# Joined value products, and products for the maxima behind the scores: an attention and expert kernel on one core

## The reference

```python
xn = layernorm(x)
# attention, 16 heads of 8 numbers
scores = Q @ K.T / sqrt(8) + 0.1 * influence     # influence = (xn We.T)(xn We.T).T, the same for all heads
attn   = softmax(scores)
att    = (attn @ V) @ Wo.T
# experts: the best 2 of 8 for every row
y      = w2[e] @ gelu(w1[e] @ xn + b1[e]) + b2[e]
out    = x + att + sum over the two experts of probability * y
```

## Time and profile before

| | before |
|---|---|
| median of 3 runs | 711.17 us |
| profiled execution | 710.7 us |
| its span, first to last instruction | 708.9 us |
| TensorE busy | 645.0 us, 91% |
| VectorE busy | 613.8 us, 87% |
| ScalarE busy | 540.8 us, 76% |
| GpSimd busy | 469.0 us, 66% |
| mean granted TensorE clock | 0.98 of 2.4 GHz |

### The profile page before, as it was taken

One profiled execution on the slowest core, in us unless ns is written; L12 is line 12 of the kernel. 1 busy time (PEld: TensorE's weight loads), 2 busy tenths in 40 slices (PEclk: granted clock), 3 DMA queues, 4 the chain that ended last, 5 costly groups with the idle time before them and its releaser, 6 DMA issues.

```text
span 708.9 us, 22900 instructions
## 1 busy us (share of the span) xinstructions
PE 645.0 (91%) x7800; PEld 431.6 (61%) x7800; DVE 613.8 (87%) x1106; ACT 540.8 (76%) x1123; POOL 469.0 (66%) x542
## 2 busy tenths in 40 slices
PE   0367899999999999879999999999999999999996
PEld 0254445555555555569999999999455555555553
DVE  8979899999899899758888888887999999999991
ACT  2583478888888888758888888888787887778785
POOL 8680478687677657125566566566688888878883
PEclk9996799999999999999999999999999999999999
DMA  9859566676686776564444454543576877788742
GB/s 249 305 161 338 150 160 180 179 204 167 178 199 178 184 183 172 148 109 100 101 106 102 101 96 110 103 99 79 142 169 174 191 186 187 175 189 195 179 112 76
DMA packets 162975, 113.71 MB, mean 160 GB/s; under 512 B 72624, under 2 KB 150448, under 8 KB 162864
## 3 DMA queue, kind: packets, MB, share of 16 engines
q1 hardware_dynamic: 153632, 90.63, 51.5%
q0 software_dynamic: 8192, 16.86, 9.8%
q10 hardware_dynamic: 1040, 4.76, 1.8%
HBM read 55.42 MB, written 47.19 MB: 145 GB/s over the span
## 4 chain that ended last, share of the span: by engine, by line
PE 62%; DVE 16%; SPq 9%; DMA 7%; issue 4%; ACT 1%; DVEq 0%; ACTq 0%
PE bank L1243 14%; PE mx L1232 13%; PE bank L1125 12%; PE bank L1103 10%; DVE mx L948 8%; PE mx L1137 6%; DMA stack<-qk_dram 4%; PE bank L1023 2%; PE bank L1185 2%; DVE A L783 2%; SPq L322 2%; DVE lo_qk L966 2%; DMA stack<-mT 2%; SPq L326 1%; PE bank L1154 1%
## 5 line engine op out<-in xcount | busy, mean ns | idle before, releaser
L700 ACT ACTIVATE A<-bank 128x512 f32<-128x512 f32 x502 | 278.0, 597 | 57.6 <-PE bank L1125 48.7
L948 DVE TENSOR_REDUCE mx<-mx 128x4 f16<-128x1024 f32 x256 | 302.5, 1205 | 18.4 <-PE mx L1137 15.9
L571 POOL TENSOR_SCALAR rows<-rows,slot_p 128x128 f32<-128x128 f32 x142 | 112.2, 800 | 99.0 <-DVE rows L999 99.0
L1125 PE MATMUL bank<-stack 113*128 113x256 f16 x1004 | 170.1, 276 | 1.8 <-ACT A L700 0.8
L557 POOL DMA_INDIRECT slots_x<-rows,pos x128 | 124.0, 969 | 50.9 <-PE bank L1125 30.0
L601 POOL DMA_INDIRECT rows<-slots_y,pos x128 | 122.0, 953 | 37.1 <-issue 18.2
L1103 PE MATMUL bank<-A,V 128*32 128x256 f32 x2048 | 137.1, 385 | 1.8 <-ACT A L700 1.7
L744 ACT ACTIVATE rows<-mx,b 128x256 f32<-128x256 f32 x284 | 111.5, 475 | 30.2 <-PE mx L1232 29.9
L1125 PEld LDWEIGHTS bank<-stack 113*128 113x128 f16 x1004 | 73.2, 97 | 89.6 <-ACT A L700 48.7
L993 DVE TENSOR_TENSOR rows<-rows 128x512 f16<-128x512 f32 x142 | 101.2, 714 | 24.5 <-ACT rows L748 22.1
L1243 PE MATMUL bank<-w,rows 128*128 x1704 | 108.4, 220 | 4.4 <-DVE rows L993 4.4
(11 more groups left out here) (142 smaller groups left out, 591.4 us busy)
## 6 DMA issues: line engine op xcount, KB each, us to landing
stack<-ctx_rest SPq DMA_DIRECT2D x64, 256.0 KB
stack<-qk_dram SPq DMA_DIRECT2D x128, 96.0 KB
slots_y<-rows SPq DMA_DIRECT2D x71, 128.0 KB, 2.1
qk_dram<-hi_qk SPq DMA_DIRECT2D x64, 128.0 KB
stack<-ctx_high SPq DMA_DIRECT2D x128, 64.0 KB
slots_x<-A ACTq DMA_DIRECT2D x1, 4644.0 KB, 19.8
w_stage<-in_w SPq DMA_DIRECT2D x8, 512.0 KB
qk_dram<-lo_qk SPq DMA_DIRECT2D x64, 64.0 KB
```

What stands on the lines that cost most here:

```text
L571: ins = pool.tensor_scalar(ye[n % 4][:, h, :], ye[n % 4][:, h, :], slot_p[:, n // 4 % 3, n % 4, h:h + 1], None, ALU.mult)
L700: act.activation(A[:, n % NA, :, :].rearrange("p h s -> p (h s)"), scores(k, n)[:, :], ACT.Exp, scale=SCALE).then_inc(s_xp, 1)
L948: dve.tensor_reduce(mx[:, a, 8 * qt:8 * qt + 8].rearrange("q (i e w) -> q i e w", i=2, e=2)[:, :, g % 2], MX[u % 2][:, :].rearrange("q (i ...
L1125: mm = pe.matmul(scores(k, n)[:, i * S:(i + 1) * S], stack[0:SHIFT + 1, par, h, 1, c * P:(c + 1) * P], stack[0:SHIFT + 1, par, h, 0, :], s ...
```

## The change

- The four groups of value products of a batch are issued in two joined pairs: groups 0 and 1 in unit 4 behind the scores, groups 2 and 3 in unit 0 of the next step, behind the scores and the output projection. (In the last step, k = 31, groups 0 to 2 stay in units 3, 5 and 7.)
- As exponentials live longer, the ring A has ten buffers in place of eight, and an exponential waits for the group that last read its buffer.
- On even units in which scores are computed, the two `plain` numbers come behind the scores and the values, not ahead of them.
- V has another layout: 48 columns for each of 16 pairs of heads, which two windows of 32 columns share, 768 columns in place of 1088. The weights of V are reordered on the host, and ScalarE's copy of V comes after the exponentials of unit 4, not of unit 3.

```diff
-NA = 8
-VB = 272
+NA = 10
+VP = 3 * 2 * DE // 2
...
-        V = sb("V", [P, 2, 4 * VB], F32)
+        V = sb("V", [P, 2, H * VP], F32)
...
-            at_ = VB * (2 * c + g % 2) - 16 * (g % 2) + 32 * (4 * (g // 2) + i)
+            at_ = VP * (8 * c + 4 * (g // 2) + i) + 16 * (g % 2)
             return V[:, par, at_:at_ + 32]
...
-                            if k != 0 or g >= 2:
-                                act.wait_ge(s_pv, 4 * b + g - 1)
+                            if 16 * b + n >= NA:
+                                act.wait_ge(s_pv, (16 * b + n - NA) // 4 + 1)
...
-                    if u == 3 and f["m"]:
+                    if u == 4 and f["m"]:
                         act.wait_ge(s_v, b1_ + 1)
...
-                    if f["m"] and u % 2 == 0:
+                    if f["m"] and u % 2 == 0 and not f["x"]:
                         for v in (u, u + 1):
                             plain(v)
                     for p in range(2):
...
                     if u == 0 and f["o"] and not closing:
-                        values(bo, paro, 3)
+                        for n in (2, 3):
+                            values(bo, paro, n)
...
-                    if u in ((3, 5, 7) if k == B - 1 else (2, 4, 6)) and f["x"]:
+                    if f["x"] and k == B - 1 and u in (3, 5, 7):
                         values(b, par, g - 1)
+                    if f["x"] and k != B - 1 and u == 4:
+                        for n in range(2):
+                            values(b, par, n)
+                    if f["m"] and u % 2 == 0 and f["x"]:
+                        for v in (u, u + 1):
+                            plain(v)
```

More of the change, by code:

```diff
@@ L184, in build @@
         stats = A[:, 0, :, :].rearrange("p h s -> p (h s)")[:, 0:NT * 6].rearrange("p (t s) -> p t s", s=6)
-        zeros = A[:, 1:NA // 2, :, :].rearrange("p n h s -> p (n h s)")[:, 0:ZROWS * RW // 2]
-        part_c = [A[:, NA // 2 + r, :, :].rearrange("p h s -> p (h s)").bitcast(F16).rearrange("p (a t) -> p a t", a=2) for r in range(4)]
+        zeros = A[:, 1:4, :, :].rearrange("p n h s -> p (n h s)")[:, 0:ZROWS * RW // 2]
+        part_c = [A[:, 4 + r, :, :].rearrange("p h s -> p (h s)").bitcast(F16).rearrange("p (a t) -> p a t", a=2) for r in range(4)]
         early = w12[:, :, :].rearrange("p a n -> p (a n)")
@@ L235, in head_values, with head_columns @@
         def head_values(par, c, g, i):
-            at_ = VB * (2 * c + g % 2) - 16 * (g % 2) + 32 * (4 * (g // 2) + i)
+            at_ = VP * (8 * c + 4 * (g // 2) + i) + 16 * (g % 2)
             return V[:, par, at_:at_ + 32]
+        def head_columns(par):
+            v = V[:, par, 0:DK]
+            return bass.AP(v.tensor, v.offset, [list(v.ap[0]), [VP, H], [32, 2], [1, DK]])
         s_x = [sem(f"s_x{q}") for q in range(4)]
@@ L485, in _ @@
             for par in range(2):
-                ins = pool.memset(V[:, par, :].rearrange("p (n j) -> p n j", n=4)[:, :, 0:256].rearrange("p n (j d) -> p n j d", d=32)[:, :, :, DK:DK + 1], 1.0)
+                ins = pool.memset(V[:, par, :].rearrange("p (n j) -> p n j", j=VP)[:, :, DK:VP:32], 1.0)
             ins.then_inc(s_post, 1)
@@ L694, in attend @@
                                 act.wait_ge(s_zero, 64)
-                            if k != 0 or g >= 2:
-                                act.wait_ge(s_pv, 4 * b + g - 1)
-                            if k == 0 and n == NA // 2:
+                            if 16 * b + n >= NA:
+                                act.wait_ge(s_pv, (16 * b + n - NA) // 4 + 1)
+                            if k == 0 and n == 4:
                                 for sm in s_cw:
                                     act.wait_ge(sm, 96)
-                            act.activation(A[:, n % NA, :, :].rearrange("p h s -> p (h s)"), scores(k, n)[:, :], ACT.Exp, scale=SCALE).then_inc(s_xp, 1)
+                            act.activation(A[:, (16 * b + n) % NA, :, :].rearrange("p h s -> p (h s)"), scores(k, n)[:, :], ACT.Exp, scale=SCALE).then_inc(s_xp, 1)
                     if u == 1 and f["p"]:
@@ L715, in attend @@
                             act.wait_ge(s_pv, 4 * b1_ - 4)
-                        act.activation(V[:, par1, :].rearrange("p (n j) -> p n j", n=4)[:, :, 0:256].rearrange("p n (j d) -> p n j d", d=32)[:, :, :, 0:DK],
-                                       MISC[:, 0:S].rearrange("p (n j d) -> p n j d", n=4, d=DK), ACT.Copy, scale=1 / WS).then_inc(s_vc, 1)
+                        act.activation(head_columns(par1), MISC[:, 0:S].rearrange("p (n e d) -> p n e d", e=2, d=DK), ACT.Copy, scale=1 / WS).then_inc(s_vc, 1)
                     if u == 2 and c_lo is not None:
@@ L1102, in values @@
                         for i in range(4):
-                            mm = pe.matmul(PV[32 * i:32 * i + 32, 0:S], head_values(pp, c, g, i), A[:, (4 * g + 2 * c + i // 2) % NA, i % 2, :],
+                            mm = pe.matmul(PV[32 * i:32 * i + 32, 0:S], head_values(pp, c, g, i), A[:, (16 * bb + 4 * g + 2 * c + i // 2) % NA, i % 2, :],
                                            start=(e == 0 and c == 0), stop=(e == 1 and c == 1))
@@ L1180, in attend @@
                     if u == 0 and f["o"] and closing:
-                        values(bo, paro, 3)
+                        for n in ((3,) if bo == B - 1 else (2, 3)):
+                            values(bo, paro, n)
                     if u == 0 and f["c"]:
@@ L1260 @@
     from concourse.bass_utils import run_bass_kernel_spmd
-    wv = np.asarray(L0_attn_Wv).reshape(2, 2, 4, DK, D).transpose(1, 0, 2, 3, 4).reshape(D, D)
+    wv = np.asarray(L0_attn_Wv).reshape(2, 2, 4, DK, D).transpose(0, 2, 1, 3, 4).reshape(D, D)
     wq, wk = (np.asarray(w).reshape(2, 2, 2, 2, DK, D).transpose(4, 0, 2, 1, 3, 5).reshape(D, D) for w in (L0_attn_Wq, L0_attn_Wk))
```

## The result

The changed kernel takes 825.97 us, the median of four runs (825.12 to 827.61); the kernel before, run beside it, 711.61. The ratio is 1.160, with a 95% interval of 1.156 to 1.165: slower by 114 us. The forecast was 811, range 775 to 860.

What follows compares the result with a forecast made beforehand. A loop through TensorE and VectorE was taken to bound the kernel, set by when each `plain` comes. Full steps add 87 us, partial ones 13, together 100 on 710.7: 811 us, range 775 to 860.

Steps and rivals of the forecast that it cites:

- the walk: One changed step timed product by product from plain 0: period 16.74 us, not 13.16 or 13.33; 811 us, chance 0.72.
- the two waits of the scratch bank: TensorE's projection waits for VectorE's addition into x (until 2.08), V's products for `lo_qk` (until 5.56), sharing one scratch bank.
- three of the ring: TensorE's second scores of units 4, 6 and 0 wait for exponentials; a bank's next score pair follows after 1.06 us.
- the loop: TensorE and VectorE waiting by turns close the period; before, via plain 1, plain 2 and maxima 2 to 7: 13.1 us.
- The links through the two tiles of maxima: `MX` has two tiles, so a `plain` waits for an earlier maximum: plain 1 for the maximum of plain 7.
- its signs: V copies 16 to 17 us apart; VectorE idle ahead of maxima 0 and 4, 1.5 to 2 us each; TensorE waits.
- The sum: Added time over all steps: 87 us in 25 full steps and 13 in six partial ones, together 100 us.
- The partial steps: Six steps at the stages' ends that lack some work, given 2.2 us each: 13 us.
- The scratch bank as a rival: Waits for the addition and `lo_qk` covered, only score ring and `MX` tiles hold TensorE: period 14.9, 760 us; chance 0.09.
- The clock as a rival: TensorE's clock falls each step at the joined values, doubling 1.7 us of work: 49 us more, 860 us; chance 0.12.
- The faster rival: TensorE's saved changes set the time: period falls to VectorE's 12.6 us, 696 us; chance 0.05.
- The edits at no cost: Ten buffers, V's new layout and its later copy, with loads and gathers, add no time; uncovered, the copy would cost 12 us.

Runs made afterwards that it cites:

- the order alone: Kernel before with one edit: on even units the products for the maxima come behind scores and values; groups, buffers, layout as before. 822.38 us, ratio 1.153.

## Why the prediction was right

**The order as the cause.** Shown: the order alone gives 109 us, the period answers as the walk has it to changes made at its links (the two waits of the scratch bank, and three of the ring, those three changed together), and the same work off the loop costs nothing. The links through the two tiles of maxima were read from the trace; no run changed them by themselves.

**The walk, link by link.** Counted from plain 0 at 641.28, the projection came at 2.17 (forecast 2.08), V's products at 5.69 (5.56), values at 7.43 (7.27), plain 4 at 9.29 (9.17), the output projection at 14.48 (14.25), the next plain 0 at 16.99 (16.74). No link failed: the walk was 0.09 us behind at the projection and 0.25 at the end of the step. The joined pair took 1.86 us (648.71 to 650.57), where 1.9 was taken. VectorE's gap of 0.56 us ahead of maximum 2 is in the walk too (3.19 to 3.71), though not among its signs.

**The sum.** 100 us forecast; the span grew by 117. Of the 17 us between them the lag of 0.25 us in 24 steps is 6. Every second step of the first stage took some 17.36 us, not 16.99: ScalarE's copies of the expert weights, which the walk left out, put off an exponential there, 0.37 us in six of the 13 steps, 2 us. One such copy, and the scores that wait behind it for 0.66 us:

```profile
146.13 1.05 ACT L730 ACTIVATE w<-w_stage 128x1024 f16<-128x1024 f32 x1
```

```profile
147.81 0.79 PE L1129 MATMUL bank<-stack 113*128 113x256 f16 x4 [0.66 <-ACT A L705]
```

Two of the 24 steps took 18.63 us by a fall of the clock, 3.3 us. The partial steps were put too low, 21 us (which takes in one full step) against 16; four more joined pairs stand there at the half clock (3.40, 3.33, 3.58 and 3.16 us where 1.93 is usual, 5.7 us together), so most of this is likely the clock too.

**The scratch bank as a rival.** Its price was right, 760 forecast and 763 measured once the two waits were taken away, and partly by luck: it took 14.9 us for every step, where the second stage had 14.75 and the first 14.68 and 15.82 by turns. The kernel as changed does wait at them.

**The clock as a rival.** It was given 0.12 and 49 us, a fall in each step. In the changed kernel it happened at six joined pairs of unit 4 (at 88.12, 105.31, 261.45, 562.05, 579.11 and 767.84 us), 9 us at most by the sum above, each at about the price forecast: a joined pair of 3.58 us where it is 1.93 otherwise, in a step of 18.63 us. TensorE at that place, and the granted clock ahead of it and in it:

```profile
579.11 3.58 PE L1107 MATMUL bank<-A,V 128*32 128x256 f32 x32
```

```profile
575.40:578.80 3.40, 1.61 (x17) 0.82 (x17) 3.32 (x5) 1.88 (x5) 2.93 (x3) 1.00 0.17 41
579.00:582.30 3.30, 3.30 (x34) 1.46 (x32) 0.31 (x2) 1.09 (x3) 2.84 (x3) 0.54 0.85 213
```

So both cases were partly true at once, and the forecast treated them as apart. The wait for the low half ahead of the fall at 579.11 was 1.31 us, longer than the usual 1.11, but ahead of the one at 261.45 it was 1.12; why some steps fall and others don't, no run here shows. Nor is the fall in the earlier trace rows the only one of the kernel before: its trace shows granted 0.50 from 307.45 to 310.80 too, between the stages. The Trainium skill (TensorE: Matmul & The Clock Gate, HAM oscillation) tells of a kernel whose clock falls in every repeat of its loop, in a wait for a DMA. The kernel with only the addition ahead comes near that, with eight of 11 steps at 17.3 to 17.95 us, though its wait is for VectorE and 1.19 us long; with the gap filled the clock over the same stretch is 1.00.

**The faster rival.** It failed as forecast: VectorE ran dry ahead of plain 0 for 1.48 us.

**The edits at no cost.** Buffers and layout cost 0.2%, less than the 1% that the forecast could tell.

## What to carry to other kernels

When several engines hand work round in order, walk one period link by link before moving an instruction: the sum of an engine's work (the change saved TensorE some 0.4 us a step by the forecast's estimate) said little here, and the moment at which the next engine runs dry gave the period. Look at what an in-order neighbour has in front of the operation that frees a shared buffer: the addition and the low half stood behind a maximum that the move made late, so a bank that had nothing to do with the move became about half of its price (63 of 114 us). And a stretch that one moves work out of may hold a wait that the work was filling.

## What was not expected of the hardware

TensorE's granted clock made a kernel with more matmuls 23 us faster (819.4 to 796.7 us): 0.44 us of repeated products a step, placed in a wait, kept it at 2.4 GHz where it had fallen to 1.2 in most steps. A change that shortens a step can so look worthless: the addition put ahead saves 0.9 us a step by the undisturbed steps, and 6.5 us of 826 by the time.
